# Attention's causal selection: the first one of every even step, from step 24 on, on VectorE

## What is computed

```python
attention = jnp.einsum('bhtd,bhkd->bhtk', q, k)           # 16 batches, 16 heads, 256 x 256
mask = jnp.where(qpos - kpos >= 0, 0.0, NEG_INF)
activation = jax.nn.softmax(attention + mask[None, None], axis=-1)
x = jnp.einsum('bhtk,bhkd->bhtd', activation, v)
...
return x + _L0_attn_ref(xn, ...) + _L0_ffn_ref(xn, ...)
```

## Time and profile before

| | |
|---|---|
| median of 3 runs | 512.21 us (511.63 to 515.35) |
| the profiled execution | 512.13 us |
| its span, first to last instruction | 510.1 us |
| busy: TensorE / VectorE / ScalarE / GpSimd | 458.3 / 350.2 / 306.4 / 296.1 us |
| mean granted TensorE clock | 0.935 |
| attention's steps | from 45 to 297 us; steps 24 to 63 from about 129 us |
| experts | from about 290 us to the end |

### The profile page before, as it was taken

One profiled execution on the slowest core, in us unless ns is written; L12 is line 12 of the kernel. 1 busy time (PEld: TensorE's weight loads), 2 busy tenths in 40 slices (PEclk: granted clock), 3 DMA queues, 4 the chain that ended last, 5 costly groups with the idle time before them and its releaser, 6 DMA issues.

```text
span 510.1 us, 12198 instructions
## 1 busy us (share of the span) xinstructions
PE 458.3 (90%) x3919; PEld 328.0 (64%) x3923; DVE 350.2 (69%) x722; ACT 306.4 (60%) x661; POOL 296.1 (58%) x424
## 2 busy tenths in 40 slices
PE   8888998989878887878898999989899999979996
PEld 4766555646555554555565667868668788858874
DVE  6796998868766565665555048757667687656897
ACT  2756776757665565665555667646547676546653
POOL 1445997968767567667677540255364497856300
PEclk9999999979998699898756699999999999989999
DMA  9786999897753454355237024767767668730762
GB/s 249 234 256 216 317 317 308 289 377 252 249 158 110 124 147 153 96 159 152 89 106 273 22 86 141 228 207 226 242 210 247 223 195 279 246 119 28 227 196 72
DMA packets 60412, 99.80 MB, mean 196 GB/s; under 512 B 11045, under 2 KB 29226, under 8 KB 59328
## 3 DMA queue, kind: packets, MB, share of 16 engines
q1 hardware_dynamic: 55872, 90.57, 56.0%
q0 software_dynamic: 4480, 8.47, 4.9%
HBM read 60.85 MB, written 38.94 MB: 196 GB/s over the span
## 4 chain that ended last, share of the span: by engine, by line
PE 65%; ACT 8%; issue 5%; SPq 5%; another core or an unknown queue 5%; DVE 4%; DMA 2%; ACTq 0%; DVEq 0%; POOL 0%
PE ps L894 11%; PE ps L892 11%; PE ps L893 10%; PE ps L1042 6%; PE ps L975 6%; PE ps L983 5%; ACT sb_work L767 3%; PE ps L1046 3%; PE ps L1025 2%; PE ps L1210 2%; SPq L494 2%; PE ps L971 2%; PE ps L1027 2%; DMA sb_ring<-qk 2%
## 5 line engine op out<-in xcount | busy, mean ns | idle before, releaser
L1416 DVE TENSOR_REDUCE sb_blockmax<-ps 128x6 f32<-128x768 f32 x128 | 121.3, 955 | 67.2 <-PE ps L983 61.9
L767 ACT ACTIVATE sb_work<-ps 128x768 f32<-128x768 f32 x128 | 104.0, 813 | 79.2 <-PE ps L971 60.8
L663 POOL DMA_INDIRECT ys<-sb_v_all,sb_xn_all x76 | 79.3, 1043 | 76.0 <-DVE sb_v_all L1543 57.1
L635 POOL TENSOR_SCALAR_AFFINE_SELECT sb_work<-sb_work 128x512 f32<-128x512 f32 x128 | 82.2, 643 | 56.1 <-ACT sb_work L767 54.7
L893 PE MATMUL ps<-sb_ring,sb_wb 128*128 128x512 f32 (+5 forms) x231 | 83.2, 360 | 0.0
L975 PE MATMUL ps<-sb_ring 32*128 32x256 f32 x256 | 53.0, 406 | 29.4 <-ACT sb_work L767 23.2
L1521 DVE TENSOR_TENSOR sb_v_all<-ps,sb_v_all 128x512 f32<-128x512 f32 (+3 forms) x93 | 57.2, 615 | 25.7 <-ACT sb_v_all L839 10.4
L613 POOL DMA_INDIRECT xs<-sb_xn_all,sb_posu x64 | 62.2, 972 | 13.7 <-issue 13.7
L975 PEld LDWEIGHTS ps<-sb_ring 32*128 32x128 f32 x256 | 26.5, 196 | 60.3 <-issue 52.1
L983 PE MATMUL ps<-sb_mask_b,sb_ident_b 128*128 128x256 bf16 x256 | 55.1, 301 | 0.0
L839 ACT ACTIVATE sb_v_all<-ps 128x512 f32<-128x512 f32 (+3 forms) x93 | 49.5, 532 | 9.0 <-PE ps L894 5.4
(11 more groups left out here) (165 smaller groups left out, 1063.0 us busy)
## 6 DMA issues: line engine op xcount, KB each, us to landing
sb_wb<-wd SPq DMA_DIRECT2D x50, 384.0 KB
sb_ring<-qk SPq DMA_DIRECT2D x64, 256.0 KB
wd<-sb_wb SPq DMA_DIRECT2D x8, 1088.0 KB, 5.2
sb_wb<-wd SPq DMA_DIRECT2D x25, 320.0 KB
xs<-sb_o_all SPq DMA_DIRECT2D x19, 260.0 KB, 3.6
qk<-sb_ring SPq DMA_DIRECT2D x32, 128.0 KB
sb_work<-ys SPq DMA_DIRECT2D x16, 256.0 KB, 3.2
sb_xn_all<-xs SPq DMA_DIRECT2D x15, 260.0 KB
```

The source lines that it names most:

```text
L635: pool.affine_select(out=o, in_=o, compare_op=ALU.is_ge, fill=0.0, base=0, pattern=[[0, 4], [1, 128]], channel_multiplier=-1)\
L663: pool.indirect_dma_start(out=ys_d, out_offset=bass.IndirectOffsetOnAxis(ap=row, axis=0), in_=yst[i % NYS][:, EMB * j:EMB * j + EMB], in_o ...
L767: act.activation(part.rearrange("p (k h q) -> p h k q", h=2, q=128), ps[:, 4:6, 0:HEAD].rearrange("p h (k q) -> p h k q", q=128), ACT.Exp, ...
L1416: dve.tensor_reduce(blockmax[:, p % 2, q, a:b + 1, 0:3], ps[:, a:b + 1, 0:HEAD].rearrange("p h (k c) -> p h k c", c=128), AX.X, ALU.max).t ...
```

## The change

A table C_KEEP of 128 columns is added to `const`: row p, column q is 3.4e38 where p <= q and 0 elsewhere. In the steps `N_KEEP` = 24, 26, ..., 62 (20 steps) GpSimd leaves its first selection out, and VectorE does it as a minimum of the weights with that table, between `projection_low` and `maximum(1)`. GpSimd's count for TensorE is lowered, and TensorE waits for VectorE's new semaphore `kept` beside it.

```diff
-C_ALL = C_DEC + ROUTED
+C_KEEP = C_DEC + ROUTED
+C_ALL = C_KEEP + 128
...
+    c[:, C_KEEP:C_KEEP + 128] = np.where(p[:, None] <= p[None, :], 3.4e38, 0.0)
...
+        N_KEEP = range(N_SEND + 1, NQ, 2)
+
+        def selected(n):
+
+            return 2 * n + 2 - len([k for k in N_KEEP if k <= n])
...
                 if isq(n):
-                    for k in range(2):
+                    for k in range(n in N_KEEP, 2):
                         pair = PAIRS[1 - k]
                         pool.wait_ge(s["ex"], 2 * n + k + 1)
...
-                    pe.wait_ge(s["sel"], 2 * n + 2)
+                    pe.wait_ge(s["sel"], selected(n))
+                    if n in N_KEEP:
+                        pe.wait_ge(s["kept"], N_KEEP.index(n) + 1)
...
                 if n in N_ROUTE:
                     next(route)
+                if n in N_KEEP:
+                    dve.wait_ge(s["ex"], 2 * n + 1)
+                    o = P[n % 2][:, HEAD * PAIRS[1][0]:HEAD * PAIRS[1][0] + 512].rearrange("p (k q) -> p k q", q=128)
+                    dve.tensor_tensor(o, o, const[:, C_KEEP:C_KEEP + 128].unsqueeze(1).to_broadcast([128, 4, 128]),
+                                      ALU.min).then_inc(s["kept"], 1)
                 if isq(m):
                     maximum(1)
```

More of the change, by code:

```diff
@@ L365, in build @@
         s_std = sem("s_std")
-        names = ("pq pk hq hk lq lk S max0 max1 mhi mx Mt q4b ST ex sel PV OT T xc rc nm busy "
+        names = ("pq pk hq hk lq lk S max0 max1 mhi mx Mt q4b ST ex sel kept PV OT T xc rc nm busy "
                  "xn xa nb xp xT xh xl V va lg tT oT wcp wsp rs var0 var rt rx selb id0 id1 cnts cnt pos tabs "
```

## The result

The changed kernel took 513.67 us (median of 12 executions, 509.59 to 517.85), the kernel before beside it 513.1 us (12 executions). The ratio that compares them is 1.0086, with an interval of 1.0049 to 1.0124: slower by 0.9%, where 513.0 / 512.21 = 1.0016 was forecast. That ratio is of the fast executions alone, so it leaves out those that are over 1.5% above the fastest of their kernel: five of the twelve of before (514.6 to 519.64 us) and two of the change's. How it weighs the others isn't on record, and plainer comparisons give less: the means of the others 1.0044, the medians of all twelve 1.0011, their means 1.0016. So the size of the loss hangs on how the executions are compared, and that there is one at all is not certain. The profiled execution took 516.33 us (span 514.6), the one of before 512.13 (510.1): 4.5 us more of span to account for.

The account below looks back on a forecast made before the run. Bound taken: the chain of exponential, second selection, two sends and TensorE's late updates. Sum: 512.13 + 0.26 (table) + 0.56 (engines meeting) = 512.95, say 513.0 us, with selections and VectorE's queue at 0; range 509.5 to 516.5.

Parts of the forecast that it names:

- Removed selections gain 0: GpSimd, even steps: 20 selections (12.7 us) go, but the sends stand behind the second selection, which waits for ScalarE; gain 0.
- The chain over the second selection and two sends: Steps 44 to 45: exponential, second selection 0.63, sends 0.97 and 0.96, then 0.94 us until TensorE's updates come through.
- Rival A: Selection behind two sends holds TensorE's updates; removed behind steps 31, 39, 47, 55: 2.6 us back, 510.4 us; chance 0.14.
- The minimum: VectorE, 20 even steps, between `projection_low` and `maximum(1)`: 0.70 us each, fits in idle time, cost 0.
- The two engines meet: VectorE's minimum and GpSimd's second selection both read SBUF; 0.28 us each in steps 28 and 44, 0.56 us in all.
- The table: `const` grows by 64 KB, loaded ahead of x's second part, for which VectorE waits: 0.26 us later.
- The pace about 4.2 us a step: Sign from step 24 on: pace stays; below 4.1 GpSimd's removed work was on the path, above 4.3 the minimum is.
- B: Rival: GpSimd is on the path throughout, so each removed selection gives its time, 12.7 us: 500.3 us; chance 0.08.
- C: Rival: minimum holds up second selection or TensorE every even step: up to 526.4 us; chance 0.10 to 515.2, 0.06 beyond 1%.
- the granted clock's term in the sum: TensorE's granted clock varies over the stretch: nothing added to the sum, only the range widened to 509.5 and 516.5 us.

Follow-up runs that it names:

- fourth session: Late condition, against the kernel before (507.37 us): itself 0.997, the change 1.0061, one send of even steps put between their selections 0.9674, second selection on VectorE 0.9718.
- first repeat: The change unaltered, run again in the first session against the kernel before (508.41 us): 508.48 us, ratio 0.9979.

## Why the prediction was right or wrong

It was wrong in the ratio: 0.2% was forecast, well within what a measurement can tell from none, and +0.86% was measured, with an interval that excludes 1.0016. In microseconds the median, 513.67, lies inside the range given, 509.5 to 516.5, and the medians of the twelve executions are 0.57 us apart where 0.8 was forecast. That the plain medians came out so close is luck as much as judgement, since 0.8 us is far below the scatter. By its steps:

- **Removed selections gain 0: right.** Idle time in front of the second selection 1.33 us (about 1.3 forecast), GpSimd's waits up by 13.1 us, and leaving the selections out gave 0.9975.
- **The chain over the second selection and two sends: right, but its last link was read too simply.** Taking one of its links away gave back 17.5 and 15.4 us; the argument hung on this chain. But I had the delay come with every pair of sends and not with a single one. Of the 24 pairs of the kernel before, four (steps 39, 47, 60 and 62) have their exponential 0.04 to 0.17 us ahead of the last send's end, the other 20 have it 0.61 to 1.38 us behind, and a single send went with 0.24 us of lateness in the fourth session. Rival A's ceiling was thus two late places (steps 31 and 55) and not four.
- **The minimum: right.** Below are the 20 minima (ns min, median, max); 0.70 us was taken. The waits show none of them right ahead of TensorE.

```profile
L1465 DVE TENSOR_TENSOR sb_work<-sb_work,sb_const x20: 680/683/694, 135.7 to 295.0; 128x512 f32<-128x512 f32 x20
```

- **The two engines meet: right in kind, too large.** 2 x 0.28 us were forecast, for steps 28 and 44. In step 44 the selection started 0.20 us before the minimum's end and took 0.70 us, 0.07 more than the earlier trace rows. In step 24, where I had the selection first, the minimum was first:

```profile
135.98 0.92 POOL L643 TENSOR_SCALAR_AFFINE_SELECT sb_work<-sb_work 128x512 f32<-128x512 f32 x1 [1.10 <-ACT sb_work L775]
...
135.73 0.68 DVE L1465 TENSOR_TENSOR sb_work<-sb_work,sb_const 128x512 f32<-128x512 f32 x1
```

  The overlap is 0.43 us and the selection 0.29 longer. All 20 steps together give 0.07 + 0.29 and 0.01 in step 36, 0.37 us, in place of 0.56. The selection became longer by the overlap less about 0.14 us, in both. The Trainium skill (SBUF — State Buffer, "Who interferes with whom") lets the second instruction wait for the whole rest of the first; by that these two would have been 0.63 us longer together, and the trace shows 0.36.
- **The table: too small to be told.** 0.26 us were forecast. VectorE's statistics start 0.04 us later than in the earlier trace rows, and step 0's first exponential 0.18 us later (45.12 us, before 44.94). But in the other profiles of the late condition it starts anywhere from 44.66 to 45.21 us, with the table or without.

```profile
7.59 0.87 DVE L1249 BATCH_NORM_STATS2 sb_stats<-sb_x_sb 128x6 f32<-128x128 f32 x4 [0.70 <-DMA sb_x_sb<-x]
```

- **The pace about 4.2 us a step: right**, 4.24, so neither A, B nor C in full.
- **Where it failed.** The step that failed is the granted clock's term in the sum, which I put at nothing: I wrote that a varying clock widens the range in us, but took the *ratio* as if both kernels had the same clock. In the profile pair 4.14 of the 4.5 us lie ahead of step 24, beside a granted clock of 0.77 in place of 0.89 from 100 to 130 us. The changed steps took 1.1 us more (0.56 forecast there), but that is within their scatter: from step 24 to step 62 the change needs 160.8, 157.3, 157.2 and 159.6 us in its four late profiles, and the kernel before 159.7 and 154.7 in two. The repeats show the same in the ratio: 0.9979, 1.0061 and 0.9986, and 0.997 for the kernel before against itself. That the 0.86% came from the clock is plausible and not shown, and its cause stays open: the clocks of the kernel before were not kept for that session beyond its profile (0.935, the one of after 0.931).
- **A wrong generality.** I read the late updates as belonging to this kernel. The other condition, without them, and 45 us faster, was not in any case of mine.

## What to carry to other kernels

Work that an engine does in front of a wait for something else is worth nothing when it goes. Look for what stands *behind* that wait in its queue, and move that into the gap instead. Here, in the late condition, moving the selections gave 0 within what can be told, moving 20 sends gave 3.3%, and both together, with the odd steps' sends moved as well, gave 5%. In the prompt condition the same 20 sends cost 1.1%, so an edit that gains by a delay has to be measured with and without it. An effect below 1% needs repeats in several sessions, with the kernel before against itself among them, and the granted clock set beside each ratio before the kernel is given the credit or the blame.

## What the hardware showed that was not expected

- The same program took 507 to 513 us in four sessions and 464 in two, on chip 4 once the one and once the other. In the late condition TensorE's updates come late beside GpSimd's sends, most of all two back to back: exponentials start 0.91, 0.94 and 0.56 us behind the last one, after ScalarE has idled for 2.0 to 2.2 us, and VectorE's maxima together with them. Behind their scores' modelled end they start up to 1.87 us. In the prompt condition's profile all 46 start 0.04 to 0.06 us behind it, 1.03 us before the last send's end in the step shown, while the sends themselves take 0.98 and 0.96 us in both. The mechanism, and whether the condition is of the chip, of the host or of other cores' work, is open.
- The sign of an edit depends on the condition: a send between the selections gave 0.9674 in the late and 1.0115 and 1.0121 in the prompt one; the second selection on VectorE 0.9718 against 1.0111 and 1.0106.
- Two engines that read SBUF at once prolong the later one by the overlap less about 0.14 us, in two cases of the changed kernel (0.20 to 0.07, 0.43 to 0.29) and four of its first repeat (0.20, 0.20 and 0.21 to 0.07, 0.46 to 0.33). The earlier trace rows fits in: 0.63 us of overlap, 0.47 longer.
